# A two-layer convolution and attention kernel: preparation rearranged, convolution output in another buffer, LayerNorm by logarithm and exponential, order tables edited

## The reference

```python
# layer 0
x_norm = _layernorm(x, norm_g, norm_b)
x_proj, z = split(x_norm @ in_proj_W)                  # 384 channels each
windows = _window_partition(x_proj, 2)                 # 4 tokens a window
y_fwd = _light_s6(windows, fwd_...)
y_bwd = flip(_light_s6(flip(windows, 1), bwd_...), 1)
y_ssm = _window_unpartition(0.5 * (y_fwd + y_bwd))
y_conv = gelu(depthwise_conv3x3(x_proj) @ pw_W)
alpha = sigmoid(gate)
y = ((alpha * y_ssm + (1 - alpha) * y_conv) * silu(z)) @ out_W
x_out = x + y
x = x_out + gelu(_layernorm(x_out) @ fuse_W1 + b1) @ fuse_W2 + b2

def _light_s6(x, ...):                                 # 8 states a channel
    dt = silu(dt_raw @ dt_W + dt_b);  a = -exp(A_log)
    state = exp(dt_t * a) * state + dt_t * b_t * x_t   # for t = 0..3
    y_t = sum_n state * c_t;  return y + x * D
# layer 1
f, g, hh = x @ Wf + bf, x @ Wg + bg, x @ Wh + bh
o = softmax(g @ f.T) @ hh @ Wo + bo
out = gamma * o + x
```

## Time and profile before

| | |
|---|---|
| runs | 4588.49, 4595.27, 4597.15 us, median 4595.27 |
| profiled execution, own time | 4591.3 us |
| its span, first to last instruction | 4589.5 us |
| layer 0 | about 33 to 2618 us of the span |
| layer 1 | about 2621 us to the end |
| PE busy in 1200 to 2400 us, in 3000 to 4589 us | 94%, 99% |
| mean granted PE clock | 0.98 |

### The profile page before, as it was taken

One profiled execution on the slowest core, in us unless ns is written; L12 is line 12 of the kernel. 1 busy time (PEld: TensorE's weight loads), 2 busy tenths in 40 slices (PEclk: granted clock), 3 DMA queues, 4 the chain that ended last, 5 costly groups with the idle time before them and its releaser, 6 DMA issues. The chain is left out here.

```text
span 4589.5 us, 78970 instructions
## 1 busy us (share of the span) xinstructions
PE 4342.8 (95%) x24064; PEld 3103.4 (68%) x24064; DVE 3790.6 (83%) x7231; ACT 3346.3 (73%) x5828; POOL 3671.6 (80%) x3475
## 2 busy tenths in 40 slices
PE   5899999999999999999999799999999999999998
PEld 3555656555556565656555588887888788888887
DVE  4899999999999999999999677777777677777775
ACT  5888898988898988898887355555555555555555
POOL 4898998989898989898989477776777677777776
...
DMA packets 139378, 198.12 MB, mean 43 GB/s; under 512 B 18458, under 2 KB 106500, under 8 KB 138756
## 3 DMA queue, kind: packets, MB, share of 16 engines
q1 hardware_dynamic: 139012, 193.76, 13.4%
...
## 5 line engine op out<-in xcount | busy, mean ns | idle before, releaser
L1355 POOL TENSOR_TENSOR pl<-probs,ph 128x512 fp32r<-128x512 f32 x1024 | 1320.2, 1291 | 547.8 <-ACT probs L1562 271.1
L805 POOL TENSOR_TENSOR dec<-dt,rates 128x384 f32<-128x384 f32 x1536 | 1513.1, 1017 | 247.8 <-ACT dt L691 192.2
L1560 ACT ACTIVATE ph<-ps_s 128x512 fp32r<-128x512 f32 x1024 | 613.8, 599 | 782.9 <-PE ps_s L1444 770.9
L1573 DVE TENSOR_REDUCE part_max<-ps_m 128x1 f32<-128x512 f32 x992 | 667.0, 688 | 339.3 <-PE ps_m L1427 339.0
L1453 PE MATMUL ps_o<-ph,values_high 128*128 128x512 f32 x2048 | 807.9, 394 | 0.1
L1453 PE MATMUL ps_o<-ph,values_low 128*128 128x512 f32 x2048 | 803.7, 392 | 0.0
L1601 DVE TENSOR_TENSOR ps_a<-probs,ps_a 128x512 f32<-128x512 f32 x992 | 682.0, 687 | 47.9 <-ACT probs L1562 40.4
L1461 PE MATMUL ps_o<-pl,values_high 128*128 128x512 f32 x2048 | 634.1, 391 | 0.0
L1562 ACT ACTIVATE probs<-ps_s 128x512 f32<-128x512 f32 x1024 | 608.9, 595 | 0.0
L969 DVE SCALAR_TENSOR_TENSOR psS<-u,bc,psS 128x384 f32<-128x384 f32 x1024 | 597.2, 611 | 1.2
L978 DVE SCALAR_TENSOR_TENSOR y_tok<-psS,bc,y_tok 128x384 f32<-128x384 f32 x960 | 552.2, 604 | 4.5
...
## 6 DMA issues: line engine op xcount, KB each, us to landing
...
xf<-in_x_dram SPq DMA_DIRECT2D x128, 128.0 KB
xb<-in_x_dram SPq DMA_DIRECT2D x128, 128.0 KB
...
out_dram<-res SPq DMA_DIRECT2D x128, 128.0 KB
```

Of the source, the lines that this page charges most:

```text
L805: last = nc.gpsimd.tensor_tensor(dec[:, q % RING, j - 1, :], dt[:, par, d, token_of(d, j), :], rates[:, d, n, :], ALU.mult)
L1355: nc.gpsimd.tensor_tensor(pl[:, m % DEPTH, :], probs[:, m % DEPTH, :], ph[:, m % DEPTH, :].bitcast(F32), ALU.subtract).then_inc(pl_ok, 1)
L1560: nc.scalar.activation(ph[:, m % DEPTH, :], ps_s[m % 2][:, :], ACT.Exp).then_inc(ph_ok, 1)
L1573: nc.vector.tensor_reduce(part_max[:, qt, kc:kc + 1], ps_m[r % 2][:, :], AX.X, ALU.max).then_inc(max_out, 1)
```

## The change

1. In a tile, LayerNorm's 1/std is made on ACT alone, as exp(-0.5 * ln(var + eps)): a second small activation, and no reciprocal on DVE (`ln1_rstd`, `ln2_rstd` are gone). Logarithm and exponential are in one function set with the scan's exponentials, and the sets are now loaded by explicit calls (`table`).
2. `own_term` is gone. For chains 7 and 8 the multiplication of z3 is written to PSUM (step m3), and z3 then adds `u * direct` to it into `dec`, so that `acc 7` and `acc 8` carry the direct terms. The list has as many steps as before.
3. POOL's backward products `umb0` to `umb3` come before `arg 5`; `acc 14` stands between `umf1` and `umf2`. On ACT `xnth` goes before `w10`, and `pw1` behind `w11`; on DVE `out1` goes before `st10` and `ln2_shift` before `st13`.
4. `conv_sb` lies over `x_win` and no longer over `y_ch`. ACT's write of it waits for `umb3` of its tile, `xk0` for `pw2` of the tile before.
5. Preparation: `A_log` is loaded into one row for each direction and spread by 16 products with a row of ones on PE; ACT takes 16 exponentials of 128x384 from PSUM. LayerNorm of tile 0 and the four DVE steps on the bias rows move from layer 0 into it; the final wait for all loads moves out of it, to the first steps that need them.
6. Layer 1: `shift_hl` is [128, 128], with the parts of the four query groups in columns 96 to 103; one transpose spreads them into 8 rows, and `shift_rows` multiplies these by `own_rows`, which is 1 where row and group belong together. The keys hold 1 in 8 rows.

PE's table is the same. Core of the diff:

```diff
 POOL_ORDER
-    arg2 arg3 umb0 acc0 arg4 acc1 arg5 umb1 umb2 acc2 arg6 acc3 arg7 acc4 arg8 umb3 acc5 arg9 acc6 arg10 acc7
+    arg2 arg3 acc0 umb0 umb1 umb2 arg4 acc1 umb3 arg5 acc2 arg6 acc3 arg7 acc4 arg8 acc5 arg9 acc6 arg10 acc7 arg11
...
+OWN_AT = (STATES - 1, STATES)
...
-    if q == STATES + 1:
-        ops += [(1, "e0"), (1, "e1")]
+    if q - 1 in OWN_AT:
+        ops[ops.index((q - 1, "z3"))] = (q - 1, "m3")
+        ops.append((q - 1, "z3"))
...
+        conv_sb = over("conv_sb", "values_high", 6144, [CB, TOK])
-        conv_sb = y_ch
...
-                    nc.scalar.activation(std1[:, :, :], mv1[:, :, 1:2], ACT.Sqrt, bias=eps[:, :]).then_inc(std1_ok, 1)
+                    table("natural_log_exp_and_others")
+                    nc.scalar.activation(std1[:, :, :], mv1[:, :, 1:2], ACT.Ln, bias=eps[:, :]).then_inc(log1_ok, 1)
+                    act.wait_ge(log1_ok, f + 1)
+                    nc.scalar.activation(std1[:, :, :], std1[:, :, :], ACT.Exp, scale=-0.5).then_inc(std1_ok, 1)
...
                 elif job.startswith("conv"):
+                    act.wait_ge(u_mul, multiplied(f, 1, T - 1))
...
                     if job == "xk0" and not (exact(f) and f == 0):
                         act.wait_ge(u_mul, multiplied(f - 1, 1, T - 1))
+                        act.wait_ge(front_full, front_job(f - 1, "pw2"))
...
-                if q == STATES:
-                    pool.wait_ge(state_ok, TILE_OPS * k + TILE_LIST.index((1, "e1")) + 1)
...
+                    elif kind == "m":
+                        nc.vector.scalar_tensor_tensor(s_t, s_t, scalar(q, t, "c"), dec[:, q % RING, T - 2, :],
+                                                       ALU.mult, ALU.mult).then_inc(state_ok, 1)
+                    elif kind == "z" and q in OWN_AT:
+                        dve.wait_ge(u_mul, multiplied(k, 1, T - 1))
+                        nc.vector.scalar_tensor_tensor(dec[:, q % RING, T - 2, :], u[:, 1, t, :],
+                                                       direct[:, par, t // (T - 1), 1, :], s_t,
+                                                       ALU.mult, ALU.add).then_inc(state_ok, 1)
...
 prepare, scalar
+                for i in range(2 * STATES):
+                    act.wait_ge(rates_made, i // 2 + 1)
+                    nc.scalar.activation(m["rates"][:, i % 2, i // 2, :], rate_banks[i % 4][:, 0:INNER],
+                                         ACT.Exp).then_inc(rates_ok, 1)
 prepare, tensor
+                for n in range(STATES):
+                    if n > 1:
+                        pe.wait_ge(rates_ok, 2 * n - 2)
+                    for d in range(2):
+                        mm = pe.matmul(rate_banks[(2 * n + d) % 4][:, 0:INNER], ones[64 * d:64 * d + 1, :],
+                                       a_rows[64 * d:64 * d + 1, n, :], start=True, stop=True)
...
 layer1
-                for qt in range(QT):
-                    mm = pe.transpose(ps_m[0][:, qt * P:(qt + 1) * P], shift_hl[:, qt, :], ident[:, :])
-                mm.then_inc(bcast_ok, 1)
+                pe.transpose(ps_m[0][:, 0:P], shift_hl[:, :], ident[:, :]).then_inc(bcast_ok, 1)
...
-                nc.vector.tensor_copy(gq[par][96:P, :], ps_m[0][96:P, :]).then_inc(max_ok, 1)
+                nc.vector.tensor_tensor(gq[par][96:P, :].rearrange("p (q n) -> p q n", q=QT),
+                                        ps_m[0][96:P, None, 0:P].broadcast_to([32, QT, P]),
+                                        own_rows[96:P, :, None].broadcast_to([32, QT, P]), ALU.mult).then_inc(max_ok, 1)
```

More of the change, by code:

```diff
@@ L40 @@
 PE_ORDER = """
-    z0 z1 yt0- yt1- yt2- z2 out0- conv0a out1- conv1a conv2a conv0b conv0c conv1c conv2c xnt0+ h2t0- h2t1- xnt1+
-    pw0 w10- xnth+ pw1 w11- proj+ pw2 inx0+ w12- inx1+ w13- inx2+ dtf0+ dtb0+ w20- inx3+ w21- dtf1+ dtb1+ inx4+
-    x1t0- dtf2+ dtb2+ x1t1- inx5+ dtf3+ dtb3+ fg0- xk0+ xk1+ xk2+ v0- bct+ v1-
+    z0 z1 yt0- yt1- yt2- z2 out0- conv0a out1- conv1a conv2a conv0b conv0c conv1c conv2c xnt0+ h2t0- h2t1- xnt1+ pw0
+    w10- xnth+ pw1 w11- proj+ pw2 inx0+ w12- inx1+ w13- inx2+ dtf0+ dtb0+ w20- inx3+ w21- dtf1+ dtb1+ inx4+ x1t0-
@@ L44 @@
+    dtf2+ dtb2+ x1t1- inx5+ dtf3+ dtb3+ fg0- xk0+ xk1+ xk2+ v0- bct+ v1-
 """.split()
 ACT_ORDER = """
-    exp1 ln1_std+ exp2 ow exp3 z0 z1 ln1_norm+ z2 exp4 ln2_std- exp5 ln2_norm- conv0c conv1c conv2c xnt0+ exp6
-    h2t0- h2t1- xnt1+ exp7 exp8 pw0 w10- xnth+ pw1 w11- exp9 proj+ exp10 pw2 inx0+ w12- inx1+ w13- exp11 inx2+
-    exp12 dtf0+ dtb0+ exp13 inx3+ exp14 dtf1+ dtb1+ inx4+ x1t0- dtf2+ dtb2+ x1t1- inx5+ dtf3+ dtb3+ exp15 fg0-
-    xk0+ xk1+ xk2+ exp0+ v0- bct+ v1-
+    exp1 ln1_std+ exp2 ow exp3 z0 z1 ln1_norm+ z2 exp4 ln2_std- exp5 ln2_norm- conv0c conv1c conv2c xnt0+ exp6 h2t0-
@@ L50 @@
+    h2t1- xnt1+ exp7 exp8 pw0 xnth+ w10- w11- pw1 exp9 proj+ exp10 pw2 inx0+ w12- inx1+ w13- exp11 inx2+ exp12 dtf0+
+    dtb0+ exp13 inx3+ exp14 dtf1+ dtb1+ inx4+ x1t0- dtf2+ dtb2+ x1t1- inx5+ dtf3+ dtb3+ exp15 fg0- xk0+ xk1+ xk2+
+    exp0+ v0- bct+ v1-
 """.split()
 DVE_ORDER = """
-    st0 ln1_stats+ st1 ln1_mean+ st2 yt0- st3 yt1- st4 ln1_rstd+ st5 yt2- st6 ln1_shift+ st7 st8 st9 out0- st10
-    out1- ln2_stats- ln2_mean- st11 st12 ln2_rstd- st13 ln2_shift- st14 st15 st16 st17 st18 st19 st20 st21 st22
@@ L61 @@
 """.split()
-RATES_BEFORE = "proj"
 CHAINS = 2 * STATES
@@ L726, in back @@
                 i = int(step[-1])
+                if step.startswith("w1"):
+                    table("gelu_and_others")
                 act.wait_ge(back_full, back_job(g, step))
@@ L743, in back @@
                                          ACT.Copy).then_inc(v_high, 1)
-            def turn_rates():
-                for d, raw in enumerate((y_tok, u)):
-                    act.wait_ge(rates_loaded, 32)
-                    src = raw[:, :, :, :].rearrange("p a t c -> p (a t c)").rearrange("p (c n) -> p n c", n=STATES)
-                    nc.scalar.activation(rates[:, d, :, :], src, ACT.Exp).then_inc(rates_ok, 1)
             def decays(k, q):
+                table("natural_log_exp_and_others")
                 act.wait_ge(arg_ok, CHAINS * k + q + 1)
@@ L772, in body @@
                 for step, tile, at in steps(ACT_ORDER, k, part):
-                    if exact(k) and k == -1 and step == RATES_BEFORE:
-                        turn_rates()
                     if step.startswith("exp"):
@@ L843, in norm_step @@
             def norm_step(what, tile, x_in, n, stats, mv, std, shift, ok, std_ok, norm_ok):
-                base = 4 * tile
+                base = 3 * tile
                 if what == "stats":
@@ L865, in front @@
             def front(step, f, par):
+                if step.startswith("ln1") and f == 0:
+                    return
                 if step.startswith("ln1") and step != "ln1_std":
@@ L1148, in _ @@
             def _(act):
+                act.preload_act_table_set("natural_log_exp_and_others")
+                for i in range(2 * STATES):
+                    act.wait_ge(rates_made, i // 2 + 1)
+                    nc.scalar.activation(m["rates"][:, i % 2, i // 2, :], rate_banks[i % 4][:, 0:INNER],
+                                         ACT.Exp).then_inc(rates_ok, 1)
+                act.wait_ge(stats1_ok, 2)
+                act.wait_ge(built, 4)
+                nc.scalar.activation(std1[:, :, :], mv1[:, :, 1:2], ACT.Ln, bias=m["eps"][:, :]).then_inc(log1_ok, 1)
+                act.wait_ge(log1_ok, 1)
+                nc.scalar.activation(std1[:, :, :], std1[:, :, :], ACT.Exp, scale=-0.5).then_inc(std1_ok, 1)
+                act.wait_ge(stats1_ok, 3)
+                for i in range(T + 1):
+                    last = nc.scalar.activation(xf[:, i, :], xf[:, i, :], ACT.Identity, scale=std1[:, i, :],
+                                                bias=shift1[:, i, :])
+                last.then_inc(m["norm1_ok"], 1)
                 act.wait_ge(loaded_first, 16 * n_first)
```

172 lines of the change are left out of this document (108 added, 64 removed).

## The result

| | before | changed |
|---|---|---|
| median of 4 runs | 4594.29 us | 4696.69 us (4694.49 to 4698.65) |
| ratio to before | 1 | 1.0223, 95% interval 1.021 to 1.0236 |
| span of the profiled execution | 4589.5 us | 4695.5 us |

The change makes the kernel slower by 2.2%. I had forecast 4571 us, a gain of 24.

The account below looks back on a forecast made before the run. Bound: in layer 0 a loop of POOL and ACT, 77.21 us a tile; in layer 1 PE. Terms -1.0 -1.2 -12.6 -8.6 -0.5 = -23.9 us: 4567.4 profiled, 4571 as median; range 4545 to 4590.

Parts of the forecast that it names:

- POOL's order: Layer 0 tiles: with POOL's steps reordered, `exp 10` comes 0.04 us earlier a tile, taken as -1 us in 30 tiles.
- quiet tile: Layer 0 tile without the extra 1.5 us of a long one; 77.2 us before, forecast 77.0 to 77.3.
- long tiles: Layer 0 tiles of 78.75 us, where the clock falls behind PE's wait for dt; 12 of 30 expected again.
- My rival: Layer 0: moved products delay the tile; `exp 8` 1.2 us later still adds 36 us, giving 4607; chance 0.08.
- Start: Before the tiles: -8.4 us for the wait for `proj_sb`, -4.2 for PE's earlier first transposes, sum -12.6.
- Layer 1: PE is the bound; three transposes fewer in 32 chunks give -8.6 us, the first chunk about 0.5 more.
- Layer 0: The tiles: -1.0 us from POOL's order and -1.2 us from the own terms, counted in the last tile only.
- The loop's POOL part: Layer 0: POOL's 46.95 us of the 77.21 us loop of POOL and ACT that sets the tile's period.
- LayerNorm at nothing: Layer 0: ACT saves 4.5 us a tile, but most turns into waits for POOL, so costed at nothing.
- own terms: Layer 0: DVE gains 1.2 us a tile but waits that much more; counted only in the last tile, -1.2 us.
- conv_sb: Layer 0: the new waits for `umb3` and `pw2` are already met and PE's table is the same: 0.
- dearer table switch: ACT, layer 0: 2.66 us a switch with a drain instead of 1.28; four would free 10.6 us a tile.

Follow-up runs that it names:

- e3: Changed kernel, POOL untouched, the shift computed by one tensor_scalar per token instead of one two-input instruction: 4542.09 us, ratio to before 0.9890.
- e1: Changed kernel with one needless wait added: umb1 waits for POOL's own umb0, opening a gap there: 4549.56 us, ratio to before 0.9907.
- e9: Changed kernel with a POOL gap ahead of the shift: acc 0 waits for arg 3 of its tile: 4552.54 us, ratio to before 0.9913.
- e10: Changed kernel with the POOL gap four instructions earlier than in e9: arg 3 waits for arg 2: 4550.83 us, ratio to before 0.9909.
- e12: Measurement behind the changed kernel: 24 POOL products without gaps, shift issued in the 14th to 18th; with wide products the 15th lets it in, the 16th doesn't.
- e7: Changed kernel, two-input shift kept, POOL's order put back nearly to that of before: 4585.99 us, ratio to before 0.9989.
- e6: Kernel before with only the shift changed, to one tensor_scalar per token: 4602.87 us, ratio to before 1.0026.

## Why the prediction was wrong

**The step that failed** is "POOL's order", its -1.0. I worked out when each step of POOL starts, and which waits of POOL and ACT move, and read the rows of POOL as time slots. I didn't ask what DVE issues meanwhile, and what the gaps were good for. `ln1_shift` stands in no term of the sum. What was wrong with it is +4.4 us a quiet tile (80.9 against 76.45 in e3, which differs in the shift alone) and some ten more long tiles; e3 is 154.6 us faster than the changed kernel. My rival had the right place ("a wait of `acc 0` or `acc 1` for z3", POOL's gap of 2.27 us) with the wrong cause, and far too small a price, 4607 us.

Three of the signs that I had named for a wrong forecast came: a gap of POOL before `acc 1`, more than 12 long tiles, and preparation that ends after 36 us.

**The cause, shown:** the long shift makes z3(1) and those behind it late, and POOL waits 2.27, 1.76 and 0.33 us at `acc 1` to `acc 3`, 4.36 together. It needs both of its causes: another form of the shift (e3) or a gap in POOL (e1, e9, e10) removes it. PE suffers too. Its convolution, behind the longer wait, takes 9.91 us in the changed kernel, with a granted clock of 0.85 there, against 8.35 in the kernel before:

```profile
1229.87 9.91 PE L509 MATMUL psF<-xp,conv_w 32*32 32x512 f32 x216 [3.60 <-ACT q_sb L724]
```

```profile
1262.55 8.35 PE L504 MATMUL psF<-xp,conv_w 32*32 32x512 f32 x216 [0.62 <-ACT q_sb L696]
```

Little of this can reach a quiet tile, since POOL's three waits alone make up nearly all of its 4.4 us; what it does to the number of long tiles was not taken apart.

The Trainium skill (SBUF — State Buffer, Who interferes with whom) says that a DVE instruction with two SBUF inputs contends with a GpSimd instruction that reads SBUF. The Trainium skill (SBUF — State Buffer, SBUF: two separate sides) says that the one of the two that starts first has the shared ports for its whole instruction, and that the other blocks. e12's 0.94 us in the 14th and 15th agree; the 8.54 us in the 16th don't, since by that rule the wait should end with one POOL instruction.

**The rest of the sum**, from e3, where the shut-out is gone (profile 50.6 us under the kernel before; 23.9 forecast for the same terms):
- Start: PE's first product dt at 48.04 against 58.99, -10.9 (48.36 and -10.6 in the changed kernel); predicted -12.6. The sum is 1.7 us off, its parts are further off. PE's 16 products for the rates take 11.4 us of PE (6.90 to 18.31 in the changed kernel), where I had counted ACT's exponentials alone and 5.9 us. So preparation ends at 37.7 and not at 33.7, and PE's first transposes come 0.6 us earlier than before (37.78 against 38.43) and not 4.2. The wait of 8.36 us is gone, as forecast, though `proj_sb` comes at 44.08 and not at 40 to 42. About 1 us more was luck: before, the eight products behind that wait took 4.44 us at a granted clock of 0.53; in the changed kernel the last eight of these twelve take 2.6 us at 1.00, which stands in no term.
- Layer 1: -9.0 in e3 and -6.5 in the changed kernel; predicted -9.1 with the first chunk. Right, within the 2.5 us by which the same instructions differ in these two profiles.
- Layer 0: -30.6, predicted -2.2. The quiet tile is 76.45 instead of 77.2, which is 22 us, and 9 instead of 12 tiles are long, 5 us. The loop's POOL part, from `umf0` to the end of `arg 10`, is 46.1 us in e3 (1214.54 to 1260.62) instead of 46.9. Three gaps of POOL that are no longer there (at `acc 15`, `arg 4` and `arg 5`) and the missing 0.24 us make up most of it: I had counted instructions and left the gaps of 0.08 to 0.14 us out. A gap put back costs a tile 0.15 to 0.3 us (e1, e9, e10).
- LayerNorm at nothing, own terms, conv_sb: e7, with all of them and the old order, has a quiet tile of 76.95, 0.25 under before. Small, as predicted, and not taken apart further. ACT is busy 993 us of 1200 in e3, 66 less than before, and it buys nearly nothing. The dearer table switch that the prediction left open is not there either: in 400 to 2400 us of the kernel before each of 361 loads has 0.02 us of idle time ahead of it and 0.01 behind it, so that a switch costs its 1.28 us and no drain.
- Long tiles: I had expected 12 again. They range from 8 to 22 over these kernels; each is worth 1.5 us, and e6 loses its 0.25 us a tile, and more, to eight more of them. What makes a tile long beyond PE's wait for dt is still open.
